# When TensorE reads the group numbers of the last five sorted chunks in a two-layer graph network kernel

## The reference, cut to what matters

```
m = gelu(h_E @ m0_w + m0_b)          # h_E: 16384 edges x 512
m = gelu(m @ m1_w + m1_b)            # 256 wide
m = gelu(m @ m2_w + m2_b)
dh = segment_sum(m, src_idx, num_segments=512) / 30
h = layer_norm(h_V + dh)             # then a 256-1024-1024-256 network, and layer_norm
...
msg = x1[dst] * x1[src]              # x1: attention over 8 heads, per node
attn_out = segment_sum(msg, dst)     # then O, layer norm, feed-forward, GRU gates
```

## Time and profile before

| what | value |
|---|---|
| three timed runs | 618.01, 620.98, 621.11 us; median 620.98 |
| the profiled execution's own time | 616.26 us |
| its span, first to last instruction | 614.2 us |
| PE busy | 591.0 us (96%), 3273 matmuls |
| PE's weight loads | 509.0 us (83%) |
| DVE / ACT / GpSimd busy | 460.1 (75%) / 366.4 (60%) / 219.6 us (36%) |
| mean granted TensorE clock | 0.994 of full |
| chain that ended last, by engine | PE 90%, DVE 6%, ACT 2%, issue 1% |

### The profile page before, as it was taken

One profiled execution on the slowest core, in us unless ns is written; L12 is line 12 of the kernel. 1 busy time (PEld: TensorE's weight loads), 2 busy tenths in 40 slices (PEclk: granted clock), 3 DMA queues, 4 the chain that ended last, 5 costly groups with the idle time before them and its releaser, 6 DMA issues.

```text
span 614.2 us, 9200 instructions
## 1 busy us (share of the span) xinstructions
PE 591.0 (96%) x3273; PEld 509.0 (83%) x3273; DVE 460.1 (75%) x790; ACT 366.4 (60%) x554; POOL 219.6 (36%) x208
## 2 busy tenths in 40 slices
PE   6999999999999999999999999998799999999895
PEld 6788888988888888898888888888788889777773
DVE  4777587777878878787887888878556566778567
ACT  4777687767677667786777776673166441411341
POOL 3055577556666455443554344510000010100001
PEclk9999999999999999999999999999899999999998
DMA  7434487385576545637456992333021304000000
GB/s 251 178 121 129 141 295 230 110 280 167 171 228 207 179 148 177 185 108 254 148 155 206 411 322 78 94 106 87 1 104 69 142 5 138 1 1 1 0 1 34
DMA packets 34075, 86.91 MB, mean 142 GB/s; under 512 B 3824, under 2 KB 23152, under 8 KB 29552
## 3 DMA queue, kind: packets, MB, share of 16 engines
q1 hardware_dynamic: 26544, 66.94, 35.0%
q0 software_dynamic: 6912, 19.10, 8.3%
q10 hardware_dynamic: 576, 0.28, 0.2%
HBM read 66.69 MB, written 19.62 MB: 141 GB/s over the span
## 4 chain that ended last, share of the span: by engine, by line
PE 90%; DVE 6%; ACT 2%; issue 1%; DMA 1%; POOLq 0%; POOL 0%; SPq 0%; DVEq 0%
PE ps L1259 28%; PE ps L1295 10%; PE ps L1441 7%; PE ps L1301 5%; PE ps L1277 5%; PE ps L1273 5%; PE ps L1272 5%; PE ps L1409 3%; PE ps L1339 3%; PE ps L1341 3%; PE ps L1343 3%; PE ps L1482 2%; PE ps L1452 2%; PE ps L1366 1%; PE ps L1471 1%
## 5 line engine op out<-in xcount | busy, mean ns | idle before, releaser
L460 POOL DMA_INDIRECT sorted_rows<-m,place x120 | 162.0, 1350 | 160.5 <-ACT m L525 132.5
L508 ACT ACTIVATE m_hi<-ps,cols 128x512 fp32r<-128x512 f32 x128 | 88.3, 690 | 73.9 <-PE ps L1259 42.0
L814 DVE TENSOR_TENSOR m_lo<-m_out,m_hi 128x512 fp32r<-128x512 f32 x128 | 88.7, 694 | 57.2 <-ACT m_out L510 45.6
L1259 PE MATMUL ps<-x_hi,w_hi 128*128 128x512 f32 x256 | 100.3, 392 | 1.1 <-DVE x_lo L699 1.1
L1259 PE MATMUL ps<-x_lo,w_hi 128*128 128x512 f32 x256 | 100.1, 391 | 0.0
L1259 PE MATMUL ps<-x_hi,w_lo 128*128 128x512 f32 x256 | 99.9, 390 | 0.0
L510 ACT ACTIVATE m_out<-ps,cols 128x512 f32<-128x512 f32 x128 | 88.0, 688 | 0.1
L699 DVE TENSOR_TENSOR x_lo<-x_raw,x_hi 128x1024 fp32r<-128x1024 f32 x64 | 75.7, 1223 | 9.4 <-ACT x_hi L502 6.6
L1295 PE MATMUL ps<-w_lo,m_hi 128*128 128x256 f32 x256 | 64.2, 283 | 0.0
L1295 PE MATMUL ps<-w_hi,m_hi 128*128 128x256 f32 x256 | 64.0, 283 | 0.0
L502 ACT ACTIVATE x_hi<-x_raw 128x1024 fp32r<-128x1024 f32 x62 | 62.2, 1058 | 1.9 <-DMA x_raw<-in_edges_dram 1.9
(11 more groups left out here) (219 smaller groups left out, 1204.0 us busy)
## 6 DMA issues: line engine op xcount, KB each, us to landing
x_raw<-in_edges_dram SPq DMA_DIRECT2D x31, 1024.0 KB
sorted_raw<-sorted_rows SPq DMA_DIRECT2D x24, 647.5 KB
d_w<-in_d_dram SPq DMA_DIRECT2D x1, 4096.0 KB
sorted_raw<-sorted_rows SPq DMA_DIRECT2D x6, 518.0 KB
rows<-in_rows_dram SPq DMA_DIRECT2D x1, 2176.0 KB, 8.3
d_w<-in_d_dram SPq DMA_DIRECT2D x2, 1024.0 KB, 4.8
sorted_rows<-m,place POOLq DMA_INDIRECT x120
w_raw<-in_w_dram SPq DMA_DIRECT2D x4, 256.0 KB, 6.9
```

Source lines behind the costliest of these rows:

```text
L460: pool.indirect_dma_start(out=sorted_d, out_offset=bass.IndirectOffsetOnAxis(ap=place[:, at:at + 1], axis=0), in_=m2[:, b % 2, t], in_offs ...
L508: nc.scalar.activation(out_hi[:, m], ps[:, bank], ACT.Gelu, bias=col(bias, m)).then_inc(hi_signal, 1)
L814: nc.vector.tensor_tensor(lo[:, m], m_out[:, m], hi[:, m].bitcast(F32), ALU.subtract).then_inc(done, 1)
L1259: last = nc.tensor.matmul(out, left, right, start=(k == 0 and i == 0), stop=(k == KE - 1 and i == 2))
```

## The change

The group numbers of chunks 25 to 29 are loaded in the loop, in blocks 26 to 30, one chunk a block, between the first half of `layer_0` and `layer_2`, and kept in registers. The chunks behind the loop use these. Chunks 0 to 24 load in front of themselves, as before, in the same blocks 26 to 30 too.

```diff
@@ sum_sorted @@
+            def groups_of(q):
+
+                sort, c, n = CHUNKS[q]
+                _, groups = nc.values_load_multi_w_load_instructions(
+                    tile_group[0:1, sort, c, 0:n], engines=[mybir.EngineType.PE], min_val=0, max_val=NC - 1)
+                return groups
+
-            def sum_sorted(q):
+            def sum_sorted(q, groups=None):
...
-                _, groups = nc.values_load_multi_w_load_instructions(
-                    tile_group[0:1, sort, c, 0:n], engines=[mybir.EngineType.PE], min_val=0, max_val=NC - 1)
+                groups = groups or groups_of(q)
                 pe.wait_ge(sorted_ready, q + 1)
@@ the order of PE @@
+            late_groups = {}
             for b in range(NBLK - 1):
                 layer_1(b)
                 layer_0(b + 1, 0)
+                if b >= NBLK - 6:
+                    q = NQ - 5 + b - (NBLK - 6)
+                    late_groups[q] = groups_of(q)
                 layer_2(b)
                 layer_0(b + 1, 1)
                 if b >= LAG_SUM:
                     sum_sorted(b - LAG_SUM)
             layer_1(NBLK - 1)
-            sum_sorted(NQ - 5)
-            sum_sorted(NQ - 4)
+            sum_sorted(NQ - 5, late_groups[NQ - 5])
+            sum_sorted(NQ - 4, late_groups[NQ - 4])
             sum_direct(DIRECT[0])
             layer_2(NBLK - 1)
             for q in range(NQ - 3, NQ):
-                sum_sorted(q)
+                sum_sorted(q, late_groups[q])
             sum_direct(DIRECT[1])
```

## The result

Eight timed runs of the changed kernel gave 613.69 to 616.73 us, median **615.24 us**, beside eight of the kernel before with a median of 619.40. The ratio is **0.9934, 95% interval 0.991 to 0.9957**: 4.1 us faster (2.7 to 5.6). A second measurement, with 12 runs against 35, gave 616.13 against 619.34 us, ratio 0.9952 (0.9924 to 0.998), 3.0 us faster (1.2 to 4.7). The forecast of 618.6 us lies above both, and the 615.24 of the first also lies 0.4 us under the lower end of the forecast's range, 615.6; the 616.13 of the second lies inside the range. The direction was right. The gain was larger than the 2.4 us of the sum in the first measurement; the interval of the second holds it.

A forecast was written before the change was run, and what follows sets the result against it. PE, busy 96% of the span, was taken to lose time to loads and DVE before the last chunks. Removed 2.4 us, added loads 0: 620.98 - 2.4 = 618.6 us, range 615.6 to 621.6.

The forecast's parts named there:

- What bounded the tail of the edges: Behind the loop PE idles before chunks 25, 26, 28 and 29, 5.0 us, waiting for register loads or DVE.
- Rival 4: Gap before chunks 28 and 29 is not the load's, so nothing is gained: 621.0 us; chance 0.05.
- The sum of the path: Along PE behind the loop, moving five loads removes 2.4 us (bounds 1.8 and 2.6); chunk 29 starts at 434.26.
- chunk 27's: Chunk 27 follows its two clearing matmuls without waiting for its load: 0.23 us more gained, together 0.42.
- The added loads at nothing: Loads added in blocks 26 to 30 cost 0 us: 17 queued matmuls give 3.9 us of cover against 3.2.
- Rival 3: Added loads in blocks 26 to 30 are not covered, PE runs dry before layer 2: 625.6 us if half covered; chance 0.07.
- The clock: Fall to 1.2 GHz at chunk 28 cost nothing before; after, a fall at chunk 26 or 29 would cost 1.5 us.
- Rival 2: Timed runs before had a fall at chunk 26 costing 1.5 us, those after none: gain 3.9, 617.1 us; chance 0.09.
- Rival 1: Clock falls once on the path, behind the wait before chunk 26 or 29: gain 0.9, 620.1 us; chance 0.20.
- The base: Forecast set against the median of the runs before, 620.98 us, not the profiled execution's 616.26.

The follow-up runs named there:

- the filled kernel: Changed kernel with nine identity products (eighteen matmuls, 2.1 us) put in front of chunks 26 and 29: 613.88 us, ratio 0.9911 to the kernel before.

## Why the prediction was right and wrong, point by point

**What bounded the tail of the edges: right.** Chunk 28 waited for its load, and chunk 26 for DVE. The start of chunk 26 was forecast at 417.15 and came at 417.08; the 0.15 us from DVE's end to the matmul stood in both places. Rival 4, that the gap isn't the load's, is gone with the idle time before chunk 28. The prediction went too far where it took the wait of chunk 28 as evidence that no matmul can be issued during a load: this chunk's matmuls take their addresses from the loaded registers and had to wait for them in any case.

**The sum of the path: right in its steps, 0.1 us too small.** Chunk 29 was forecast at 434.26 us and stands at 434.12 in the filled kernel, and the products behind direct block 31 start at 443.14 instead of 445.67, 2.53 us earlier than in the profile of before, where the fall cost nothing. The last matmul of direct block 31 was forecast at 441.8 and starts at 441.69 there. A term that was mis-sized is chunk 27's: from the first clearing matmul to the chunk's second it took 0.88 us before (427.86 to 428.74) and takes 0.56 after (429.09 to 429.65), 0.32 won and not 0.23, and the total is 2.5 instead of 2.4.

**The added loads at nothing: right.** There is no idle time in blocks 26 to 30, all five loads had the forecast 17 matmuls of cover, and the kernel that has them alone is within its interval of no change. Rival 3 is excluded.

**The clock: the step that failed.** The prediction said that the fall in front of chunk 28 "cost nothing, since chunk 29 waited for its load anyway", and from this one fall it concluded that a fall would be something new on the path after the change. Both come from reading one execution as the kernel. The 0.51 us before chunk 29 in the earlier trace rows was short because the low clock had stretched chunk 28; at full clock that gap is 2.0 us, as the kernel with chunk 26's gap filled shows. So the kernel before had three gaps of two microseconds, not two, and the change took away one of the pair. When the low clock reached over chunk 29 it cost 1.8 us. So the term that the sum put at nothing, what falls cost before the change, was in truth 2.8 us in the median (619.37 against 616.54 filled; 3.4 from the 619.97 of the same series), and what they cost after it was 1.5 (615.34 against 613.88; 2.3 from the 616.13 of the second measurement). The difference, with the path's 2.5, makes the gain. That it comes to some 4 us proves nothing, since the same medians stand on both sides; what shows the two parts is that the lowest runs are 2.5 us apart, and that each kernel gets faster when its gaps are filled. The size of the clock's share isn't known better than 0.5 to 2 us: the two measured gains, 3.0 and 4.1, less 2.5, give 0.5 and 1.6, and the fillings 1 to 2. Why a fall is dear in some runs and free in others stays open. Rival 2 named the right direction with a chance of 0.09, but as luck of single runs and not as a share of the change. Rival 1, to which I gave 0.20, happened in the profiled run, and 15 of the 20 unfilled runs after the change had a clock under 0.999; but falls cost the kernel before more.

**The base: 1.6 us of the miss.** The forecast of 618.6 lies 3.4 us over the measured 615.24. The median of three runs, 620.98, was itself 1.6 us over that of eight, which is scatter of a kernel with four levels; the other 1.8 us is the gain. Against the 619.40 of the eight runs the same sum gives 617.0. The profiled run, 616.26 us, stood on the lowest of the four levels and the median of three near the highest. Its distance of 4.7 us was noted in the prediction and not asked about, and the question would have led to what the steps cost.

## What to carry to other kernels

A register load in front of short work left TensorE idle for 2.0 of its 2.8 us here; with 17 matmuls of a layer still to run it was free. Before a fall of the clock is called harmless, look at the clocks of several runs and ask how long the gaps beside it are when the work between them runs at full speed. Where a wait can't be removed, matmuls that fit into it with room to spare won 1.4 to 3.4 us here, and too many in front of a load pushed it back and lost it all. They don't replace the better order of work: the change gave 2.5 us that no filling gave.

## What the runs showed of the hardware that was not expected

- In the loop the register loads (all 25 of the kernel before, and the ten from 346.9 us on in the changed one) started with about 17 matmuls left to run. 24 short matmuls in front of a load delayed it to when about 18 of them were left, by some 1.3 us; with 8 in front the chunk came no later before chunks 26 and 28, and 0.2 us later before chunk 29.
- Runs of one kernel lay on steps of 1.5 to 1.9 us, most of them with a mean clock about 0.003 lower. Falls were seen at three places: in the first block near 13 us, where PE waited for x_lo (idle 2.27, 2.44, 2.45 and 2.47 us in the four profiles with a fall there, at most 2.12 in those without), behind chunk 26's gap, and at chunks 28 and 29.
- A gap of 2.0 us was sometimes followed by a low clock (2.04 before chunk 28) and sometimes not (2.01 before chunk 26, in the same execution). Where products filled it and left 0.3 to 1.3 us open, no profile shows a fall behind it.
